# Four graph layers on one core: the product of memberships as two float32r matmuls per graph instead of one float32 matmul

## The reference, cut to what matters

```python
H  = (adj != 0).astype(x.dtype)
w  = adj.reshape(N, -1)[:, :C]                 # adj's first row
Dn = 1 / einsum('nce,ne->nc', H, w)            # 0 where the sum is 0
Be = 1 / H.sum(axis=1)                         # 0 where the sum is 0
m  = Be[:, :, None] * einsum('nce,nch->neh', H, xw)
out = Dn[:, :, None] * einsum('nce,neh->nch', H, m) + b
```

## Time and profile before

| | |
|---|---|
| runs of the kernel before | 1374.58, 1376.95, 1377.8 us; median 1376.95 |
| span of the profiled execution, first to last instruction | 1374.0 us |
| that execution's own time | not given apart from its span; the three runs lie 0.6 to 3.8 us above it |
| PE, PEld (weight loads) | 1334.7 us (97%), 1289.6 us (94%) |
| DVE, ACT, POOL | 1238.5 (90%), 1000.8 (73%), 996.9 us (73%) |
| mean granted TensorE clock | 0.993 of full speed |

### The profile page before, as it was taken

How to read it: one execution, slowest core, us unless ns; L and a number is a source line. 1 busy time by engine, 2 the same in 40 slices (tenths; PEclk the granted TensorE clock), 3 DMA queues, 4 the chain that set the end, 5 groups by cost and what they waited for, 6 DMA issues and landing times.

```text
span 1374.0 us, 32347 instructions
## 1 busy us (share of the span) xinstructions
PE 1334.7 (97%) x10772; PEld 1289.6 (94%) x10772; DVE 1238.5 (90%) x3863; ACT 1000.8 (73%) x2376; POOL 996.9 (73%) x2005
## 2 busy tenths in 40 slices
PE   4899999999999999999999999999999999999996
PEld 3799999999999999999999999999999999999985
DVE  5799999999999999999999999999999999999974
ACT  3677777777777777777777777777777777777763
POOL 4677777777777777777777777777777777777741
PEclk8999999999999999999999999999999999999999
DMA  7011111111112112111111111101111111111000
GB/s 195 23 33 55 41 43 55 44 40 55 48 36 55 48 36 55 47 36 55 48 36 55 50 33 55 56 28 55 55 32 51 55 32 51 55 32 36 29 9 24
DMA packets 83220, 64.49 MB, mean 47 GB/s; under 512 B 40304, under 2 KB 65520, under 8 KB 83056
## 3 DMA queue, kind: packets, MB, share of 16 engines
q1 hardware_dynamic: 83056, 62.43, 16.2%
HBM read 45.62 MB, written 16.78 MB: 45 GB/s over the span
## 4 chain that ended last, share of the span: by engine, by line
PE 93%; DVE 2%; POOL 1%; ACT 1%; SPq 1%; issue 1%; DMA 1%; DVEq 0%; POOLq 0%
PE BANK L323 30%; PE BANK L291 24%; PE BANK L330 15%; PE WIDE L323 8%; PE WIDE L302 8%; PE WIDE L330 4%; PE BANK L341 2%; PE BANK L276 2%; DMA X_B<-in_xs 1%; SPq L226 0%; DVE BN_C L497 0%; ACT H_D L370 0%; DVE BN_B L497 0%; DVE Z_B L585 0%; ACT UHI_D L401 0%
## 5 line engine op out<-in xcount | busy, mean ns | idle before, releaser
L401 ACT ACTIVATE UHI_B<-BANK 128x512 fp32r<-128x512 f32 x96 | 57.3, 597 | 46.2 <-PE BANK L291 46.2
L401 ACT ACTIVATE UHI_C<-BANK 128x512 fp32r<-128x512 f32 x96 | 57.3, 596 | 43.8 <-PE BANK L291 43.8
L401 ACT ACTIVATE UHI_D<-BANK 128x512 fp32r<-128x512 f32 x96 | 57.3, 597 | 43.1 <-PE BANK L291 42.8
L401 ACT ACTIVATE UHI_A<-BANK 128x512 fp32r<-128x512 f32 x96 | 57.3, 597 | 43.1 <-PE BANK L291 43.1
L538 DVE TENSOR_TENSOR ULO_D<-BANK,UHI_D 128x512 fp32r<-128x512 f32 x96 | 64.6, 673 | 16.1 <-ACT UHI_D L401 16.1
L538 DVE TENSOR_TENSOR ULO_B<-BANK,UHI_B 128x512 fp32r<-128x512 f32 x96 | 64.6, 673 | 11.2 <-ACT UHI_B L401 11.2
L538 DVE TENSOR_TENSOR ULO_C<-BANK,UHI_C 128x512 fp32r<-128x512 f32 x96 | 64.6, 673 | 10.9 <-ACT UHI_C L401 10.9
L538 DVE TENSOR_TENSOR ULO_A<-BANK,UHI_A 128x512 fp32r<-128x512 f32 x96 | 64.7, 674 | 10.0 <-ACT UHI_A L401 10.0
L673 POOL TENSOR_TENSOR LN_B<-LN_B,MHALF 128x2 f32<-128x2 f32 x80 | 55.9, 699 | 1.3
L673 POOL TENSOR_TENSOR LN_D<-LN_D,MHALF 128x2 f32<-128x2 f32 x80 | 55.5, 694 | 1.3
L673 POOL TENSOR_TENSOR LN_A<-LN_A,MHALF 128x2 f32<-128x2 f32 x80 | 55.5, 694 | 1.3
(11 more groups left out here) (486 smaller groups left out, 5728.2 us busy)
## 6 DMA issues: line engine op xcount, KB each, us to landing
X_A<-in_xs SPq DMA_DIRECT2D x16, 256.0 KB, 3.0
X_B<-in_xs SPq DMA_DIRECT2D x16, 256.0 KB, 2.9
X_C<-in_xs SPq DMA_DIRECT2D x16, 256.0 KB, 2.9
X_D<-in_xs SPq DMA_DIRECT2D x16, 256.0 KB, 2.8
out_rows<-O_A SPq DMA_DIRECT2D x16, 256.0 KB, 2.0
out_rows<-O_B SPq DMA_DIRECT2D x16, 256.0 KB, 2.1
out_rows<-O_C SPq DMA_DIRECT2D x16, 256.0 KB, 2.0
out_rows<-O_D SPq DMA_DIRECT2D x16, 256.0 KB, 2.1
```

What stands on the lines that cost most here:

```text
L401: nc.scalar.activation(UHI[s][:, 0:J * D], bank(s, step, k)[:, :], ACT.Copy).then_inc(sem(f"c{step}"), 1)
```

## The change

`HT` becomes float32r (zeros and ones are exact in it). `BHT` is replaced by two float32r tiles, `BHI` with the rounded values and `BLO` with what rounding left. The first row is loaded into a tile of its own, `ROW`. A new DVE step "TS" (`members_split`) rounds `BE` and the first row and subtracts to get their rests; ACT "B" scales `HT` by both parts, four activations in place of two; PE "G" adds two float32r matmuls per graph. ACT "B" now waits for "TS" in place of POOL's `be_ready`, and the load of the first row waits for `row_split` in place of `pG`.

```diff
-    "T": 3.90, "X": 4.63, "XA": 14.25, "DA": 18.63, ...
+    "T": 3.90, "X": 4.63, "TS": 16.00, "XA": 14.25, "DA": 18.63, ...
...
-        BHT = per_stream("BHT", J, P + 2)
+        ROW = per_stream("ROW", J, 1)
+        BHI = per_stream("BHI", J, P + 2, dt=F32R)
+        BLO = per_stream("BLO", J, P + 2, dt=F32R)
-        HT = per_stream("HT", J, P)
+        HT = per_stream("HT", J, P, dt=F32R)
...
             def load_first_row(s, group, n):
                 if n is not None:
-                    sp.wait_ge(sem("pG"), n)
-                sp.dma_start(BHT[s][:, :, P:P + 1], adj_t[...])
+                    sp.wait_ge(sem("row_split"), n)
+                sp.dma_start(ROW[s][:, :, :], adj_t[...])
...
             def incidences(s, c, k):
-                pe.wait_ge(sem("first_row_loaded", s), c["dma"])
+                pe.wait_ge(sem("row_split"), c["n1"])
                 pe.wait_ge(sem("bht_ready"), c["n1"])
                 bank_free(s, "G", k)
                 for j in range(J):
-                    last = nc.tensor.matmul(bank(s, "G", k)[...], HT[s][:, j, :], BHT[s][:, j, :], start=True, stop=True)
+                    dst = bank(s, "G", k)[:, j * (P + 2):(j + 1) * (P + 2)]
+                    nc.tensor.matmul(dst, HT[s][:, j, :], BLO[s][:, j, :], start=True, stop=False)
+                    last = nc.tensor.matmul(dst, HT[s][:, j, :], BHI[s][:, j, :], start=False, stop=True)
...
             def by_members(s, c, k):
-                act.wait_ge(sem("be_ready"), c["n1"])
-                for j in range(J):
-                    last = nc.scalar.activation(BHT[s][:, j, 0:P], HT[s][:, j, :], ACT.Copy, scale=ST[s][:, BE, j:j + 1])
+                act.wait_ge(sem("be_split"), c["n1"])
+                for part, share in ((BLO, ST[s][:, BEL, :]), (BHI, BES[s][:, :].bitcast(F32))):
+                    for j in range(J):
+                        last = nc.scalar.activation(part[s][:, j, 0:P], HT[s][:, j, :].bitcast(F32), ACT.Copy,
+                                                    scale=share[:, j:j + 1])
...
+            def members_split(s, c, k):
+                dve.wait_ge(sem("first_row_loaded", s), c["dma"])
+                if k:
+                    dve.wait_ge(sem("pG"), c["n1"] - len(STREAMS))
+                dve.wait_ge(sem("be_ready"), c["n1"])
+                row, row_hi, row_lo = ROW[s][:, :, 0], BHI[s][:, :, P], BLO[s][:, :, P]
+                nc.vector.tensor_copy(BES[s][:, :], ST[s][:, BE, :]).then_inc(sem("be_high"), 1)
+                nc.vector.tensor_copy(row_hi, row).then_inc(sem("row_high"), 1)
+                dve.wait_ge(sem("be_high"), c["n1"])
+                nc.vector.tensor_tensor(ST[s][:, BEL, :], ST[s][:, BE, :], BES[s][:, :].bitcast(F32), ALU.subtract)\
+                    .then_inc(sem("be_split"), 1)
+                dve.wait_ge(sem("row_high"), c["n1"])
+                nc.vector.tensor_tensor(row_lo, row, row_hi.bitcast(F32), ALU.subtract).then_inc(sem("row_split"), 1)
...
-                nc.gpsimd.memset(BHT[s][:, :, P + 1], 1.0)
+                nc.gpsimd.memset(BHI[s][:, :, P + 1].bitcast(F32), 1.0)
+                nc.gpsimd.memset(BLO[s][:, :, P + 1].bitcast(F32), 0.0)
```

More of the change, by code:

```diff
@@ L118, in program @@
         VE, NMU, RSTD, NB = range(4)
-        ST = per_stream("ST", 13, J)
-        CNT, CNM, BE, DNM, DNI, DN, S2, DG1, DINV, SC, S8, RSR, RSA = range(13)
+        ST = per_stream("ST", 14, J)
+        BES = per_stream("BES", J, dt=F32R)
+        CNT, CNM, BE, DNM, DNI, DN, S2, DG1, DINV, SC, S8, RSR, RSA, BEL = range(14)
         RR = per_stream("RR", J)
@@ L184, in load_first_row @@
                 if n is not None:
-                    sp.wait_ge(sem("pG"), n)
-                sp.dma_start(BHT[s][:, :, P:P + 1], adj_t[group, STREAMS.index(s), :, :, 0:1], allow_slow_non_contiguous=True)\
+                    sp.wait_ge(sem("row_split"), n)
+                sp.dma_start(ROW[s][:, :, :], adj_t[group, STREAMS.index(s), :, :, 0:1], allow_slow_non_contiguous=True)\
                     .then_inc(sem("first_row_loaded", s), 16)
@@ L275, in incidences @@
                 for j in range(J):
-                    last = nc.tensor.matmul(bank(s, "G", k)[:, j * (P + 2):(j + 1) * (P + 2)], HT[s][:, j, :], BHT[s][:, j, :],
-                                            start=True, stop=True)
+                    dst = bank(s, "G", k)[:, j * (P + 2):(j + 1) * (P + 2)]
+                    nc.tensor.matmul(dst, HT[s][:, j, :], BLO[s][:, j, :], start=True, stop=False)
+                    last = nc.tensor.matmul(dst, HT[s][:, j, :], BHI[s][:, j, :], start=False, stop=True)
                 last.then_inc(sem("pG"), 1)
@@ L628, in last_out @@
                 nc.vector.tensor_tensor(O[s][:, :, :], bank(s, "6W", k)[:, :], RES[s][:, :, :], ALU.add).then_inc(sem("c6W"), 1)
-            parts = {"X": stats(X, "0"), "XA": aggregate("0"), "T": members,
+            parts = {"X": stats(X, "0"), "XA": aggregate("0"), "T": members, "TS": members_split,
                      "DA": degrees, "DB": degrees_inverse, "DC": degrees_positive, "DD": shift_scale, "0W": hidden,
@@ L685, in with_loops @@
                 pool.wait_ge(sem("ht_ready"), c["n1"])
-                nc.gpsimd.tensor_tensor(AT[s][:, :, :], HT[s][:, :, :], pair(OFFDIAG[:, :]), ALU.mult)\
+                nc.gpsimd.tensor_tensor(AT[s][:, :, :], HT[s][:, :, :].bitcast(F32), pair(OFFDIAG[:, :]), ALU.mult)\
                     .then_inc(sem("at_offdiag"), 1)
```

## The result

The changed kernel takes 1385.38 us (median of 4 runs, 1385.22 to 1385.49) against 1375.76 us for the kernel before (4 runs): a ratio of 1.0069, 95% interval 1.0056 to 1.0081, 9.6 us more. The forecast was 1381.3 us, 4.3 more than the 1376.95 us known then, with a range of 1377 to 1391. Its start term is there; 5 us more come from the steady part, which had been costed at nothing.

A forecast was written before the change was run, and what follows sets the result against it. PE was taken to bound the kernel, busy for all of the 20.44 us period. 0 on PE, 0 in the steady part and +4.3 at the start, on 1376.95 us, gave 1381.3 us, range 1377 to 1391.

The forecast's parts named there:

- PE's product at 0: PE step "G": four float32r instructions a pair at 111.5 ns, 0.446 us as before, a change of 0.
- the 0.44 to 0.46 us named as a sign: Sign in the changed profile: the pieces of PE step "G" still last 0.44 to 0.46 us.
- Columns don't set the pace: Denies the rival that columns pace PE's narrow float32r products: -8.6 us with the start, 1368.4 us, chance 0.08.
- narrow float32r slow: Rival on PE's product: narrow float32r costs as much as whole float32, +28.5 us plus the start, 1409.8 us, chance 0.11.
- estimate by passes alone: PE's product counted by passes through the array: two in place of four, 14.3 us less.
- The start at +4.3: Start of the kernel: "TS" behind the weight setup on DVE delays PE's first products and 1U(A), 4.3 us more.
- The steady part at 0: Repeated periods: added DVE and ACT work fits into idle time, costed at 0.
- chain DVE, ACT, PE comes late: Rival in the steady part: spare 0.5 us used up, 0.1 us a pair, +6.4 + 4.3, 1387.7 us, chance 0.07.
- the 1.28 us of idle time: ACT's idle time before its relu at 699.91, waiting for DVE's H_C; counted as cover for added work.
- The spare time of 0.42 us in front of RES_D: DVE's idle time before RES_D, counted to absorb the up to 0.38 us of delay behind "TS".

The follow-up runs named there:

- wide product: Changed kernel with 256 columns in each of PE's float32r products in place of 130, the others unused: 1385.63 us.
- float32 product: Changed kernel, but PE multiplies by the rounded part alone, as one float32 matmul per graph, leaving the rest out: 1383.01 us.
- early split: Changed kernel with first-pass "TS" earlier in DVE's list: stream A's before the weight setup, B's between two of the last weight splits: 1380.09 us.
- split on GpSimd: Changed kernel with the four small instructions of the split done by GpSimd, DVE's list as in the kernel before: 1384.47 us.
- ACT twice: Kernel before with ACT's scaling of the memberships done twice, first into a tile nobody reads: 1375.66 us.
- one product and no split: Kernel before with one float32r matmul per graph on the rounded part, rounding on ACT, no rest formed and no added DVE instruction: 1375.68 us.
- one product: Changed kernel with the matmul of the rest left out, one float32r matmul per graph: 1382.47 us.

## Why the prediction was right in its range and wrong in a term

**PE's product at 0.** Right, and for the reason given: a narrow float32r matmul is one instruction and one load, and loads come at 0.11 us. "G" and the step behind it went from 0.445 + 0.891 to 0.395 + 0.941 us; "G" by itself is shorter than the 0.44 to 0.46 us named as a sign, because 0.05 us moved into the next step. The two rivals on its price are out. Columns don't set the pace: four matmuls, at 61 ns each, would have taken 0.24 us, and 0.395 + 0.050 were taken. Nor is narrow float32r slow. The estimate by passes alone, 14.3 us less, from the Trainium skill's FP8 and Floating Point Precision (TensorE Precision Notes), did not come; its 107 ns for a load of 128 columns (TensorE: Matmul & The Clock Gate, LDWEIGHTS) is near the 111 measured. One product instead of two takes "G" from 0.395 to 0.173: at 130 columns the number of loads counts. At 256 columns (wide product) "G" and 6U take 0.475 + 0.891, 0.03 us more.

**The start at +4.3.** Right in each link, too small in two. DVE's W2G instruction waited for its weights until 10.10 us (9.28 before), so WLO0W started 0.8 us later than assumed, which carries over to 1U(A). That is chance, as over the 14 traces this start lies between 9.15 us (wide product) and 10.54 (float32 product). And PE's first eight shift products took 3.62 us in place of 2.78. In the kernel before, these products, and 1U(A) as a window (busy by engine, granted clock):

```profile
12.55 2.78 PE L252 MATMUL WIDE<-W,SPREAD 128*128 128x256 f32 x8
...
32.27:35.70 3.43, 3.43 (x16) 3.43 (x17) 1.25 (x5) 1.11 (x3) 2.83 (x4) 0.50 0.01 2
```

The starts of the shift products are 0.43 us apart up to 14.26 us before and up to 21.49 us in the changed kernel, and 0.21 to 0.22 us apart from 14.52 and 21.90 us on. The first entry of TensorE's granted clock in the two traces, 1.00 (2.4 GHz), begins at 14.34 and 21.88 us. In front of it the pace is that of the lower level, 1.2 GHz: 0U(A) there has 0.215 us from start to start, as 1U(A) has at a granted clock of 0.50. PE had worked without a gap since 10.71 us before and since 16.24 us in the changed kernel. So five of the eight products started at the lower level before, and all eight and the one behind them in the changed kernel; the sum took them as equally long. The two delays add 1.7 us at BW and all behind it (24.48 against 22.75, G_B at 37.25 against 35.55, 1U(A) at 38.14 against 36.4). By the fourth "1U" 5.2 us are left, and the early split, which moves only this, is 5.3 us faster than the changed kernel.

**The steady part at 0.** Wrong: 0.085 us a pair, 4.8 us. The step that failed is "I cost the steady part at 0", which weighed "G" and the waits around it but took PE's other steps as fixed. In the changed kernel PE hardly waits (0.368 us against 0.366 for the step itself), and still needs more: its float32r steps go at a slower pace more often, 0.12 us a pair, and the 0.04 us of waits that the kernel before had in front of 4W are gone. That the two narrow products are enough for this, with DVE's list as before, is shown by the split on GpSimd. The whole loss, 9.6 us, is more than twice the 4.3 of the sum. The time lies in the range because the range left room for a late chain of up to 0.15 us a pair; that a steady loss of such a size came by another way is luck. The median of three runs, from which the sum started, was also 1.2 us above that of four, which makes forecast and measured time look nearer than the two differences are.

**The rival "chain DVE, ACT, PE comes late".** Its size was near (0.1 us a pair), its place was not. ACT's extra work is free (ACT twice), as the 1.28 us of idle time in the earlier trace rows said. The spare time of 0.42 us in front of RES_D shrank to 0.25 us (median). But the way over conv_out to 4W, of which no row of the forecast told, is at 20.58 to 20.60 us with the split in DVE's list, level with what PE needs now; with one product and no split it is at 20.515 at most, though 5W, 2W and 3W, which lie on it, went at the slower pace there. That DVE's added 0.34 us reach it over the tanh and GpSimd's additions was argued from the traces and not tried by itself. So removing PE's cost alone gives little: 2.4 us with the float32 product, and 2.9 with one product, of which 1.2 are at the start. Two limits stand near the same height, and each alone costs a like amount: 57 x 0.071 = 4.0 us with one product, 57 x 0.121 = 6.9 us with the split on GpSimd. An engine that is idle for 1.3 us in a period is not thereby free; what counts is the way from 3W to 4W, on which DVE idles for 0.03 us between RES_D and conv_out in the changed kernel.

**Still open.** Why two narrow float32r products make the pace change sides, and why the start address of HT and the tiles behind it decides it, modulo 256 bytes as far as these runs go, no run shows. Which of those tiles it is was not tried, nor an addition on GpSimd moved in the changed kernel itself.

## What to carry to other kernels

Before a cheaper step on the bounding engine is credited, look for the second limit: here the 0.22 us saved on PE came back as waits in front of 4W (one product), and showed only when one addition on GpSimd was moved out of the way of a DVE instruction. An instruction that takes three times its neighbour's time with the same shape is such a place, and one line in the order of GpSimd was worth 13 us, a quicker pace on PE included. And an experiment that adds a tile also moves the addresses of those behind it: keep these fixed, or its time is not that of the edit.

## What the runs showed of the hardware

- A float32r matmul with 256 columns took 113 or 118 ns from start to start, whole steps at one pace; with 512 columns 233 or 229 ns, and the runs with the quicker one there had the slower one in 5W, 2W and 3W. A shift of tiles by 128 bytes changed it (1362.69 against 1357.27 us). With two narrow float32r products between two blocks of such steps, and tiles placed as before modulo 256 bytes, the second block took the other pace than the first in 224 of 224 periods.
- A DVE instruction with two inputs in SBUF took 1.35 us in place of 0.41 while GpSimd added two tiles in SBUF; the two-column ST<-G, with one input, was held too, 0.43 us on average in place of 0.15 us, until GpSimd's addition ended.
- One float32r product, with the rest left out, and GpSimd's addition moved runs in 1357.27 us with tiles placed as before modulo 256 bytes, 0.9866 of the kernel before, its period 20.20 us in the window:

```profile
606.50:626.70 20.20, 20.20 (x169) 19.67 (x168) 18.21 (x61) 15.44 (x39) 15.31 (x32) 1.00 0.17 47
```
